# Expert tiles: rows of the second tile copied first, a late table in four parts, a last block without GpSimd's drain

## The reference, cut to what matters

```python
x = conv_attention(x, ...)                     # 4 images of 256 channels, 32 x 32
t = to_tokens(x)                               # 4 x 1024 tokens of 256
t = t + attention(layernorm(t), ...)           # 8 heads
t = t + ffn(layernorm(t), ...)                 # the stage that is changed
return from_tokens(t, x)

def ffn(x, Wr, br, W1, b1, W2, b2):            # E = 8 experts, D = 256, H = 1024
    route_prob = softmax(xt @ Wr + br)
    routes = argmax(route_prob)                # one expert for each token
    for e in range(E):
        h = gelu(xt @ W1[e] + b1[e])
        y = h @ W2[e] + b2[e]
        out += y * (routes == e)
    return out * (p_max / stop_gradient(p_max))    # a factor of 1
```

## Time and profile before

| | |
|---|---|
| median of 3 runs | 1191.05 us (1190.48 to 1195.1) |
| the profiled execution | 1192.07 us, of which its span 1190.2 us |
| busy in the span: TensorE, its weight loads | 1106.0 us (93%), 817.5 us (69%) |
| VectorE, ScalarE, GpSimd | 713.0 (60%), 469.7 (39%), 677.9 us (57%) |
| DMA queue of SyncE (hardware), of GpSimd (software) | 131.25 MB, 41.84 MB |
| mean granted clock of TensorE | 0.954 |

### The profile page before, as it was taken

How to read it: one execution, slowest core, us unless ns; L and a number is a source line. 1 busy time by engine, 2 the same in 40 slices (tenths; PEclk the granted TensorE clock), 3 DMA queues, 4 the chain that set the end, 5 groups by cost and what they waited for, 6 DMA issues and landing times. The chain is left out here.

```text
span 1190.2 us, 24360 instructions
## 1 busy us (share of the span) xinstructions
PE 1106.0 (93%) x7846; PEld 817.5 (69%) x7847; DVE 713.0 (60%) x1523; ACT 469.7 (39%) x556; POOL 677.9 (57%) x686
## 2 busy tenths in 40 slices
PE   6898999899689999999999999999876999999995
PEld 3586878778455555555555555556756899999995
DVE  3265757657757777777777777760574544444442
ACT  2303232131225555555555555555551222232231
POOL 0155444263337777777777777783057455555553
PEclk8799999989779999999999999999888999999998
DMA  7335465636171323232323232314678666566561
GB/s 218 98 107 182 163 212 182 252 106 221 48 267 40 97 61 97 60 97 62 97 62 97 62 97 62 97 33 125 248 287 254 212 209 229 202 212 220 199 224 36
DMA packets 69677, 173.67 MB, mean 146 GB/s; under 512 B 12768, under 2 KB 33184, under 8 KB 68992
## 3 DMA queue, kind: packets, MB, share of 16 engines
q1 hardware_dynamic: 56336, 131.25, 34.4%
q0 software_dynamic: 13296, 41.84, 10.3%
HBM read 117.16 MB, written 52.45 MB: 143 GB/s over the span
## 5 line engine op out<-in xcount | busy, mean ns | idle before, releaser
L225 DVE TENSOR_REDUCE s_nmax<-ps_v 128x1 f32<-128x512 f32 x484 | 311.6, 686 | 115.9 <-PE ps_v L219 106.4
L1088 POOL TENSOR_TENSOR h_added<-h_added,h_expd 128x1024 f32<-128x1024 f32 x124 | 295.5, 2383 | 38.2 <-ACT h_expd L1111 30.4
L1111 ACT ACTIVATE h_expd<-ps_v 128x1024 f32<-128x1024 f32 x128 | 131.0, 1023 | 154.9 <-PE ps_v L1137 150.2
L1984 PE MATMUL ps_h<-xs_c,lnt 128*128 128x128 f32 x1248 | 149.4, 279 | 5.6 <-DVE xs_c L1917 3.8
L1984 PEld LDWEIGHTS ps_h<-xs_c,lnt 128*128 128x128 f32 x1248 | 146.0, 196 | 6.8 <-issue 4.1
L1151 PE MATMUL h_ps_o<-h_expd,s_vh 128*32 128x256 f32 x2048 | 137.9, 387 | 0.0
L1111 ACT ACTIVATE h_expd<-h_ps_e 128x1024 f32<-128x1024 f32 x128 | 130.4, 1018 | 0.0
L653 PE MATMUL a_ps_v<-a_val,a_expd 128*128 128x257 f32 x512 | 120.6, 389 | 5.8 <-ACT a_expd L524 4.5
L653 PEld LDWEIGHTS a_ps_v<-a_val,a_expd 128*128 128x128 f32 x512 | 98.5, 194 | 24.3 <-ACT a_expd L524 6.5
L2035 ACT ACTIVATE hid<-ps_h 128x1024 f32<-128x1024 f32 x39 | 39.9, 1024 | 188.4 <-DVE ps_h L1910 188.4
L1838 POOL TENSOR_TENSOR pause<-pause 128x1 f32<-128x1 f32 x156 | 53.2, 341 | 103.6 <-DVE ys L1935 92.6
(11 more groups left out here) (258 smaller groups left out, 2018.1 us busy)
## 6 DMA issues: line engine op xcount, KB each, us to landing
lnt<-in_w SPq DMA_DIRECT2D x39, 1024.0 KB, 4.9
qk_scr<-a_head_hi SPq DMA_DIRECT2D x14, 512.0 KB, 4.0
qk_scr<-a_head_lo SPq DMA_DIRECT2D x14, 512.0 KB, 5.5
a_w_qk<-in_w POOLq DMA_DIRECT2D x24, 256.0 KB, 4.0
w_scr<-a_w_hi POOLq DMA_DIRECT2D x24, 256.0 KB, 2.5
w_scr<-a_w_qk POOLq DMA_DIRECT2D x24, 256.0 KB, 3.1
w_hi<-w_scr SPq DMA_DIRECT2D x8, 768.0 KB, 4.4
w_lo<-w_scr SPq DMA_DIRECT2D x8, 768.0 KB, 9.9
```

The lines of the kernel that those rows point to most:

```text
L225: self.nc.vector.tensor_reduce(self.nmax[k][:, nb, half:half + 1], ps_m[:, half, :], AX.X, ALU.max, negate=True).then_inc(self.v_max, 1)
L1088: nc.gpsimd.tensor_tensor(total[:, :], (expd[:, 0, :] if m == 1 else total[:, :]), expd[:, m, :], ALU.add).then_inc(g_add, 1)
L1111: nc.scalar.activation(expd[:, m, :], flat(ps_e[m % 2]), ACT.Exp, scale=SCALE).then_inc(a_exp, 1)
L1984: last = nc.tensor.matmul(ps_h[k][:, c // 4, c % 4 * P:(c % 4 + 1) * P], w1_now[k][:, t, c * P:(c + 1) * P], xs_c[:, t, :], start=(t == 0) ...
```

## The change

Three edits. In VectorE's program the copy of tile 1's rows (`tokens(1)`) now comes ahead of the biases of tile 0 (`biased(0, 0)`). The late table is made in LATE_PARTS = 4 pieces, after tiles 0, 1, 2 and 3: the counts; the scan; the five instructions of `place` that give `texp_i`; the eight that give `start_i`. So tiles 3 and 4 are straight code too and the first loop over pairs starts at 2. The last block is opened with `no_gpsimd_drain=True`.

```diff
--- before.py
+++ after.py
@@ -1292,6 +1292,7 @@
 READY_IMAGES = 2
 READY = READY_IMAGES * NB - (E - 1)
 SCANNED = 1
+LATE_PARTS = 4
 
 
 class Schedule:
@@ -1346,7 +1347,7 @@
             step(vec.tensor_tensor(base[1 - c][:, shift:E], base[c][:, shift:E], base[c][:, 0:E - shift], ALU.add))
             c, shift = 1 - c, 2 * shift
 
-    def place(self, dve, ntile, rows, keep, first, n):
+    def place(self, dve, ntile, rows, keep, first, n, parts=(0, 1)):
 
         step, vec, base = self.stepped(dve), self.nc.vector, self.base
         over_e = lambda ap: ap.rearrange("p (t o) -> p t o", o=1).to_broadcast([P, n, E])
@@ -1354,11 +1355,14 @@
         tiled, tiled2, end = self.tiled[:, 0:n, :], self.tiled2[:, 0:n, :], self.end
         texp, start, tile_no = self.texp[:, first:first + n], self.start[:, first:first + n], keep["tile_no"][:, 0:n]
         c = SCANNED
-        step(vec.tensor_tensor(end[:, :], base[c][:, :], ntile[:, :], ALU.add))
-        step(vec.tensor_tensor(tiled, over_e(tile_no), over_t(end[:, :]), ALU.is_ge))
-        step(vec.tensor_reduce(texp, tiled, AX.X, ALU.add))
-        step(vec.tensor_scalar(texp, texp, float(E - 1), None, ALU.min))
-        vec.tensor_copy(self.texp_i[:, first:first + n], texp).then_inc(self.v_experts, 1)
+        if 0 in parts:
+            step(vec.tensor_tensor(end[:, :], base[c][:, :], ntile[:, :], ALU.add))
+            step(vec.tensor_tensor(tiled, over_e(tile_no), over_t(end[:, :]), ALU.is_ge))
+            step(vec.tensor_reduce(texp, tiled, AX.X, ALU.add))
+            step(vec.tensor_scalar(texp, texp, float(E - 1), None, ALU.min))
+            vec.tensor_copy(self.texp_i[:, first:first + n], texp).then_inc(self.v_experts, 1)
+        if 1 not in parts:
+            return
 
         step(vec.tensor_tensor(tiled, over_e(tile_no), over_t(base[c][:, :]), ALU.subtract))
         step(vec.tensor_scalar(end[:, :], ntile[:, :], -1.0, 0.0, ALU.add, ALU.max))
@@ -1381,15 +1385,17 @@
 
     def late(self, dve, keep, have, part):
 
-        if part:
-            self.place(dve, self.ntile, self.rows, keep, READY, TILES - READY)
+        if part >= 2:
+            self.place(dve, self.ntile, self.rows, keep, READY, TILES - READY, parts=(part - 2,))
+            return
+        if part == 1:
+            self.scan(dve, self.ntile)
             return
 
         self.tiles_of(dve, self.ntile, have, keep, full=False)
         step, vec = self.stepped(dve), self.nc.vector
         step(vec.tensor_tensor(self.ntile[:, :], self.ntile[:, :], self.used[:, :], ALU.subtract))
         step(vec.scalar_tensor_tensor(self.rows[:, :], self.used[:, :], float(P), keep["region"][:, :], ALU.mult, ALU.add))
-        self.scan(dve, self.ntile)
 OUTPUT_CONSTS = 8
 
 
@@ -1778,7 +1784,7 @@
                 row = eng.value_load(pad_pos[0:1, e:e + 1], min_val=0, max_val=E * REGION - P)
                 eng.dma_start(io["xs_scr"][bass.ds(row, P), :], keep["padding"][:, :]).then_inc(padded, 16)
 
-        with nc.Block() as block:
+        with nc.Block(no_gpsimd_drain=True) as block:
 
             @block.sync
             def _(sp):
@@ -1946,14 +1952,14 @@
                 dve.wait_ge(v_experts, 1)
                 dve.wait_ge(bias_in, 32)
                 tokens(0)
+                tokens(1)
                 biased(0, 0)
-                tokens(1)
                 rest(0, 0)
                 tile(0, first=True)
-                for n in range(2):
+                for n in range(LATE_PARTS):
                     schedule.late(dve, keep, prior[:, B, :], n)
-                    tile(n + 1, parity=1 - n, nth=n, first=(n == 0))
-                for some in ((1, EARLY_PAIRS), (EARLY_PAIRS, PAIRS)):
+                    tile(n + 1, parity=(n + 1) % 2, nth=(n + 1) // 2, first=(n == 0))
+                for some in ((LATE_PARTS // 2, EARLY_PAIRS), (EARLY_PAIRS, PAIRS)):
                     if some[0] == EARLY_PAIRS:
                         dve.wait_ge(v_experts, 2)
                     with dve.Fori(*some) as p:
```

## The result

The changed kernel takes 1178.8 us (median of 4 runs, 1175.6 to 1181.6), the kernel before 1193.1 us (4 runs with the later one, 1190.5 to 1196.4). The ratio is 0.9896, 95% interval 0.987 to 0.9922. The measured time lies 1.8 us above the predicted 1177.0 and inside the range of 1175.8 to 1181.8; the gain between the medians is 14.25 us. The profiled execution took 1178.39 us, 13.68 less than that of before.

What follows compares the result with a forecast made beforehand. TensorE, busy almost throughout, was taken as the bound, with a drain in the tail; 0.38 (swap) + 4.42 (table) + 9.27 (drain) = 14.07 us, giving 1177.0 us, range 1175.8 to 1181.8.

Steps and rivals of the forecast that it cites:

- The drain: Last block: taking out GpSimd's DRAIN after the last scatter gains 9.27 us; other bound zero.
- Rival (a): End of program: drain is moved past the span, not removed; gain 4.8, time 1186.25 us; chance 0.13.
- The table: Tiles 0 to 4: four pieces of late table work on VectorE give back 4.42 us; bounds 2.0 and 4.42.
- Pieces 0 to 2: VectorE after tiles 0 to 2: 2.2 to 2.36 us each fit the 2.22 idle; cost zero, bounds 0 and 0.14 each.
- the swap: Start, tiles 0 and 1: earlier copy of tile 1's rows gains 0.38 us net; bounds 0.94 and -0.53.
- Piece 3: Ahead of tile 6's first layer: 3.86 us long, 0 net cost, bounds 0 and 0.31.
- up to 1 us more: Piece 3 beside GpSimd's DMAs: by the skill's exclusion rule the sum would be up to 1 us worse; not adopted.
- the wait of 2.2 us brings the clock down: Tile 4: TensorE's stall lowers its granted clock to 0.50, making the first layer 1.66 us slower.
- tile 8's wait: Tile 8: TensorE's 0.27 us wait for weights mostly hides piece 3's 0.3 us.
- the bound of -0.53: Swap's worst case: ScalarE's chain already decides and the biases' whole 0.53 us delay goes on.
- (b): Drain goes but table pieces overrun, clock falls again, swap gives nothing: gain 11.3, time 1179.8 us; chance 0.16.
- (c): Tiles 0 to 6: short stalls keep TensorE's clock at 0.50, 3 us per tile, time 1198 us; chance 0.03.

Runs made afterwards that it cites:

- e2: Kernel before, only without GpSimd's drain in the last block: 1181.4 us, ratio 0.992.
- e4: Kernel before with only the late table in four parts: ratio 0.9964.
- e11: e6 plus a third buffer for tile 2's first-layer weights and padding rows written early: 1176.6 us, ratio 0.9877.
- e1: Kernel before with the swap alone (copy of tile 1's rows ahead of tile 0's biases): ratio 0.9998.
- e12: The changed kernel again, unaltered, on the chip of the last variants: 1177.5 us, ratio 0.9899.
- e5: Changed kernel with tile 0's expert number loaded into VectorE's register ahead of the wait of tile 1's copy: ratio 0.9879.
- e10: e6 plus early padding: two padding rows' writes after each tile's loads from tile 2 on: 1177.8 us, ratio 0.9895.
- e6: e5 plus ScalarE's gelu table loaded ahead of the phase: ratio 0.9886.
- e8: Kernel before with three in-place GpSimd products between the last scatter's landing and the drain: 1203.9 us, ratio 1.0107.
- e7: Kernel before with GpSimd's drain at the end of all four blocks: ratio 1.0021.
- e3: Changed kernel with the swap undone: ratio 0.9889.

## Why the prediction was right, and where it was not

**The drain.** Forecast 9.27, measured 9.17 (e2). Rival (a) falls by the 1.79 us between span and time. The Trainium skill (Runtime: NRT & Kernel Launch, section "The ~15µs preamble/postamble breakdown") has the runtime wait for all engines after a kernel; of the drain left out nothing showed up there.

**The table.** Forecast 4.42, measured 4.34 to 4.41 (after, e4). Pieces 0 to 2 cost nothing at all. The 0.07 between the two is the swap's, behind tile 0. Piece 3 cost 0.1, not 0.31. It is 3.78 us long (937.88 to 941.66) where I took 3.86: its second instruction takes 0.17 us instead of 0.43, and the idle for the reload 0.76 instead of 0.57. Of before and of after:

```profile
927.30 0.99 POOL L1841 DMA_INDIRECT t_rows<-t_scr,id_in  x1 [0.30 <-issue]
...
927.86 0.43 DVE L1364 TENSOR_SCALAR tab_end<-tab_ntile 128x8 f32<-128x8 f32 x1
```

```profile
937.88 0.40 DVE L1367 TENSOR_TENSOR tab_tiled<-tile_no,tab_base 128x240 f32<-128x240 f32 x1
938.31 0.17 DVE L1368 TENSOR_SCALAR tab_end<-tab_ntile 128x8 f32<-128x8 f32 x1
...
941.66 1.23 DVE L1916 TENSOR_TENSOR ps_h<-ps_h,b_t 128x1024 f32<-128x1024 f32 x1 [0.76 <-issue]
```

That small difference does not explain the 0.2 us; the rest is open. The old instruction ends with the gather that GpSimd runs beside it (927.86 + 0.43 = 928.29 = 927.30 + 0.99), to 0.01 us in all five traces of the old table. The Trainium skill (SBUF — State Buffer, section "SBUF: two separate sides") has a VectorE instruction with two SBUF inputs and one of GpSimd exclude each other, from which I had worked out up to 1 us more. The traces do not bear that microsecond out: the instructions with two inputs over 128x240 took 0.40 to 0.44 us, no more beside a scatter or a gather than without. The one that ended with the gather has a single input, and in e11 it took 0.21 beside a scatter; what held it is open. (Nor did the old eight instructions lie beside two of GpSimd's DMAs, as I wrote: the gather lay beside them, the scatter beside the five ahead.)

What I took as given is that the wait of 2.2 us brings the clock down (1.66 of the 4.10 in the sum). By e1, which has the wait without the low clock, 1.5 of the 4.1 are the clock's. They are gone with the wait, so the sum stood; but they belong to four of the five traces of the old table, not to the wait as such.

**The swap: the step that failed.** I put the first biases at 0.53 later and took the expert's number as loaded. The first biases' load had run at 901.1, under the first layer, before and now runs at 907.0, behind the copy's wait, and is itself longer. The load's rows, of before and of after:

```profile
L1903 DVEq TENSOR_LOAD <-tab_texp_i x1: 557/557/557, 901.1 to 901.1; - x1
```

```profile
L1909 DVEq TENSOR_LOAD <-tab_texp_i x1: 752/752/752, 907.0 to 907.0; - x1
```

With the range check behind it that puts the biases 1.35 after where they were, not 0.53 (908.18 - 906.52 against 908.07 - 907.76). The prediction wrote of this reload for the table's pieces ("each piece ends with a wait, behind which VectorE loads the next expert's number again") and did not apply it to the wait that the swap itself moves. The term was +0.38 and is -0.62 (-0.43 in e12), below the bound of -0.53 that I gave; e5 gives the load its old cover back and then has 5.51 where the forecast had 5.41 (913.17 - 907.76).

**Tile 8.** I let piece 3 vanish in tile 8's wait. That wait is not a constant: the tiles from 4 to 9 take 23.45 to 24.65 us over the 14 traces. Of the 0.45 us lost here between before and after, 0.12 is piece 3, which did not vanish; 0.2 is TensorE's late load ahead of tile 6's second layer and the rest tile 8's wait for weights, and both of these vary between traces with the same table.

**The sum.** 14.07 forecast, 14.25 between the medians and 13.68 in the profiled executions look closer than they are: that is in part luck. The change itself is 12.44 by the phase's lengths. The swap was a full microsecond worse than forecast and tiles 4 to 9 took 0.45 more, and 1.24 came from stages that the change does not touch. The ratio's interval, a gain of 9 to 15.5 us, holds all of these. Of (b) only "the swap gives nothing" came true, and worse; the table gave what the sum had. (c) had no part: TensorE was granted 1.00 from 905 to 1170.

## What to carry to other kernels

Moving a wait forward in an engine's queue moves everything behind it, register loads too: look at what the engine's sequencer had done under cover of the old order, and load it ahead of the new wait. TensorE's 0.7 us in e10 look like the same thing, and the timeline shows them as idle without a releaser. A gain ahead of one tile is only a gain if the next transfer is early enough; after e6 the weights of tile 2 were the bound. And measure sub-microsecond edits by lengths between two rows of the same trace, since programs that are equal up to a point reach it at 898 to 903 us.

## What the runs showed that I had not expected

- GpSimd's drain takes 9.2 us after 192 transfers (the same with 11 us of work between the last landing and the drain, e8) and 7.1 after 86 with drains ahead of these (e7). Leaving it out at the end of the program takes the whole of it off the measured time (e2).
- The same wait of TensorE ahead of tile 4 (2.2 to 2.4 us) was followed by 3.4 us at a granted clock of 0.50 in before, e2, e7 and e8 and by none in e1; the nine traces with four parts have none there.
- An undisturbed tile takes 6.793 us in eight of the 14 traces and 6.780 in the others (e3, e6, e8 to e11), 0.39 us over 29 tiles; no edit goes with it, and the granted clock is 1.00 in both.
